# Expert layer on one Trainium2 core: two adds per turn moved to later search rounds, gathers queued ahead of scatters

## What is computed

```
def balanced_assignment(scores):          # scores: 8192 rows x 8 experts
    for e in range(E):
        s = jnp.where(taken, -jnp.inf, scores[:, e])
        _, idx = jax.lax.top_k(s, C)      # C = 1024 rows for each expert
        taken = taken.at[idx].set(True)
...
norm = layer_norm(feat, ln_g, ln_b)
sort_by_expert = balanced_assignment(norm @ centroids.T)
routed = feat[sort_by_expert].reshape(E, C, D)
h = layer_norm(routed, ln_g, ln_b)
h = gelu(einsum('ecd,edf->ecf', h, w1) + b1)      # D = 128, F = 512
h = einsum('ecf,efd->ecd', h, w2) + b2
out = routed + h                                   # back to the rows' places
```

## Time and profile before

| | us |
|---|---|
| median of 3 runs | 1326.44 (1326.17 to 1327.94) |
| the profiled execution, its own time | 1329.28 |
| its span in the trace (first to last instruction) | 1326.4 |
| PE busy | 1122.2 (85%) |
| DVE busy | 878.6 (66%) |
| POOL busy | 775.3 (58%) |
| ACT busy | 677.6 (51%) |
| mean granted TensorE clock | 0.914 of full |

### The profile page before, as it was taken

How to read it: one execution, slowest core, us unless ns; L and a number is a source line. 1 busy time by engine, 2 the same in 40 slices (tenths; PEclk the granted TensorE clock), 3 DMA queues, 4 the chain that set the end, 5 groups by cost and what they waited for, 6 DMA issues and landing times. The chain is left out here.

```text
span 1326.4 us, 34010 instructions
## 1 busy us (share of the span) xinstructions
PE 1122.2 (85%) x11612; PEld 734.3 (55%) x11612; DVE 878.6 (66%) x2747; ACT 677.6 (51%) x1452; POOL 775.3 (58%) x829
## 2 busy tenths in 40 slices
PE   4999999999999996647998994869999635999996
PEld 1444444444444443434776773759998324677674
DVE  7677777777777775777788602765556768777720
ACT  3777766777776764401433453575555400343353
POOL 2878887877888785102555674645554102466675
PEclk8999999999999998856999997879999755999998
DMA  8000000000000000410221223200000410122221
GB/s 193 2 1 0 0 0 0 0 0 0 0 0 0 0 1 2 144 33 21 60 58 56 79 72 95 59 1 0 0 0 0 135 42 19 47 61 61 61 84 40
DMA packets 55851, 47.32 MB, mean 36 GB/s; under 512 B 13142, under 2 KB 47190, under 8 KB 55772
## 3 DMA queue, kind: packets, MB, share of 16 engines
q1 hardware_dynamic: 44748, 27.92, 7.6%
q0 software_dynamic: 8192, 17.84, 4.8%
q10 hardware_dynamic: 2832, 0.54, 0.3%
HBM read 28.44 MB, written 17.83 MB: 35 GB/s over the span
## 5 line engine op out<-in xcount | busy, mean ns | idle before, releaser
L349 POOL TENSOR_TENSOR patt_aa<-patt_aa,causal_aa 128x512 f32<-128x512 f32 x256 | 319.3, 1274 | 73.4 <-DVE patt_aa L528 71.5
L528 DVE TENSOR_TENSOR patt_aa<-p_second_aa,first_aa 128x512 f32<-128x512 f32 x384 | 247.5, 686 | 133.9 <-ACT first_aa L424 130.5
L424 ACT ACTIVATE first_aa<-p_first_aa 128x512 f32<-128x512 f32 x384 | 208.6, 596 | 135.9 <-PE p_first_aa L627 132.1
L627 PE MATMUL p_second_aa<-q_t_aa,k_t_aa 32*128 32x512 f32 x768 | 234.8, 641 | 0.0
L627 PE MATMUL p_first_aa<-q_t_aa,k_t_aa 32*128 32x512 f32 x768 | 217.1, 641 | 15.1 <-ACT first_aa L424 14.8
L1423 POOL DMA_INDIRECT rows_e<-norm_rows,index_e x128 | 124.5, 973 | 163.7 <-DVE index_e L1119 126.5
L646 PEld LDWEIGHTS p_z_aa<-patt_aa,v_aa 128*32 128x32 f32 x3072 | 72.2, 109 | 147.5 <-issue 79.6
L1386 ACT ACTIVATE hid_e<-p_h_e,b_e 128x512 f32<-128x512 f32 x128 | 88.6, 692 | 116.3 <-PE p_h_e L1255 116.3
L1255 PE MATMUL p_h_e<-rows_t_e,w_e 128*128 128x512 f32 x256 | 144.5, 675 | 0.1
L1340 PE MATMUL p_cnt_e<-reach_e,ones_e 128*128 128x120 bf16 x896 | 84.6, 250 | 69.7 <-DVE reach_e L1183 69.5
L1376 ACT ACTIVATE rows_t_e<-p_t_e,bias,gain 128x512 f32<-128x512 f32 x32 | 24.9, 779 | 210.7 <-PE p_t_e L1246 210.7
(11 more groups left out here) (260 smaller groups left out, 2065.4 us busy)
## 6 DMA issues: line engine op xcount, KB each, us to landing
norm_rows<-norm_n SPq DMA_DIRECT2D x32, 288.0 KB, 2.8
w_e<-L_ffn_w SPq DMA_DIRECT2D x32, 256.0 KB
x<-L_attn_a_x SPq DMA_DIRECT2D x8, 512.0 KB, 5.4
x<-ffn_rows SPq DMA_DIRECT2D x7, 512.0 KB, 6.8
rows_e<-norm_rows,index_e POOLq DMA_INDIRECT x128, 2.6
ffn_rows<-yb_e,index_e POOLq DMA_INDIRECT x64
out<-yb_e,index_e POOLq DMA_INDIRECT x64
x<-ffn_rows SPq DMA_DIRECT2D x2, 256.0 KB, 3.2
```

The costliest lines, as they stand in the source:

```text
L349: pool.tensor_tensor(patt[n % LAG][:, b, :, :], patt[n % LAG][:, b, :, :], causal[:, None, :].broadcast_to([P, 4, P]), ALU.mult).then_inc( ...
L424: act.activation(first[n % 2][:, b, :], p_first[b][:], ACT.Identity).then_inc(first_copied, 1)
L528: dve.tensor_tensor(patt[n % LAG][:, b, :, :].rearrange("p h q -> p (h q)"), p_second[(2 * n + b) % ROOMS][:], first[n % 2][:, b, :], ALU. ...
L627: pe.matmul(out[:], k_t[par][rows, half, keys * P:(keys + 1) * P], q_t[par][rows, half, :, queries * P:(queries + 1) * P], start=True, sto ...
```

## The change

Two edits, both in `experts`. `add_back(e-3, 0)` goes from the window of round 2 to that of round 5 (the sixth), and `add_back(e-3, 1)` from round 4 to round 7 (the eighth). On GpSimd, a turn with one list does its gather first and its scatters behind it.

```
                     if e >= 3:
-                        windows[2].append(lambda: add_back(e - 3, 0))
-                        windows[4].append(lambda: add_back(e - 3, 1))
+                        windows[5].append(lambda: add_back(e - 3, 0))
+                        windows[7].append(lambda: add_back(e - 3, 1))
...
                 def turn(e, par, half):
                     _, lists, compute = does(e)
                     last = len(lists) > 1
+                    if lists and not last:
+                        gather(lists[0], 1 - par)
                     if compute and (not isinstance(e, int) or e > 2):
                         for h in range(2):
                             scatter(e - 3, 1 - par, half, h)
                             if last:
                                 gather(lists[h], lists[h] % 2)
-                    if lists and not last:
-                        gather(lists[0], 1 - par)
```

## The result

| | before | after |
|---|---|---|
| median, us | 1326.79 (1326.17 to 1327.94, 5 runs) | 1333.23 (1332.09 to 1334.29, 5 runs) |
| ratio to before | | 1.0044, 95% interval 1.0032 to 1.0055 |
| span of the profiled execution | 1326.4 | 1331.9 |
| PE, DVE, POOL busy, us | 1122.2, 878.6, 775.3 | 1121.2, 876.4, 772.2 |
| mean granted clock | 0.914 | 0.921 |

Measured again beside other executions of the kernel before (median 1325.64), the changed kernel took 1333.27 us: 1.0057, interval 1.0044 to 1.0070. So it is slower by 6 to 8 us, where 3.6 was forecast. The forecast's direction stands; the measured median lies 0.4 us above its range (the forecast started from a median of 1326.44, and 1.0044 times that is 1332.3, just inside).

What follows compares the result with a forecast made beforehand. Neither TensorE nor VectorE alone was taken to bound a searching turn; GpSimd's queue was nearly full from turn 6. Terms 0.05 + 0.23 + 0.3 + 2 x 1.5 gave 3.6 us slower, median 1330.0, range 1326.0 to 1332.8.

Steps and rivals of the forecast that it cites:

- Parts 1 and 2: Search turns: moving the adds from rounds 2 and 4 gains 0.60 and 0.20 us, so a turn lasts 26.09.
- Part 4: GpSimd's queue: twelve scatters between gathers of experts 5 and 6 delay turn 8; layers end 0.05 and 0.23 us later.
- Part 5: Scatters in rounds 1 and 2 slow VectorE: 0.04 us for each of eight turns, 0.3 in all.
- Part 6: TensorE's clock falls behind turn 8's wait of 3.4 us, costing 1.5 us in each layer.
- The sum: Whole kernel: the terms add to 3.6 us slower, span 1330.0 and median 1330.0.
- step from span to median: Whole kernel: a difference found in the traced span, 3.6 us, is added unchanged to the median of 1326.44.
- GpSimd's queue isn't the bound: Turn 8: expert 6's rows land within 34.9 us of expert 5's `index`, the gains stand, 1319.8 us; chance 0.06.
- GpSimd starves: Search: twelve scatters at 1.26 + 0.30 us each make expert 6 3.4 us later per layer, 1336.8; chance 0.04.
- The adds uncovered: Rounds 5 and 7: adds not hidden, a turn loses 1.2 and gains 0.8 us, 1333.2 in all; chance 0.05.

Runs made afterwards that it cites:

- turn-6 kernel: Kernel before, adds left in rounds 2 and 4, gather put ahead of the scatters in turn 6 alone: 1336.76 us, ratio 1.0083.
- turn 6 split: Changed kernel, but in turn 6 scatter half 0, gather, scatter half 1, with the first add in round 4: 1320.67 us, ratio 0.9965.
- order only: Kernel before, adds left in rounds 2 and 4, only GpSimd's order changed to gather first: 1340.28 us, ratio 1.0106.
- turn 6 as before: Changed kernel, with turn 6's adds and GpSimd order put back as in the kernel before: 1333.43 us, ratio 1.0039.
- adds only: Kernel before, only the adds moved to rounds 5 and 7, GpSimd's order kept: 1382.70 us, ratio 1.0428.
- wait filled: Changed kernel, plus 64 matmuls with unread results on TensorE ahead of turn 8's first transposes: 1329.62 us, ratio 1.0025.
- two split kernels: Changed kernel with the gather between the scatter halves and the first add in round 4, in turn 6 (1320.67 us) or turns 3 to 6 (1321.37 us).

## Why the prediction was right, and where its sizes were off

**Parts 1 and 2, the search.** Right. Turn 3, which has no scatters in its first rounds, lasts 26.06 for the 26.09 forecast, and VectorE's count in round 5 now waits for the add. The prediction credited the first layer's turns 3 to 5 with 2.68 us, though its own 0.80 a turn gives 2.40; they gained 2.46.

**Part 4, GpSimd's order.** The mechanism, the place and its being the bound were right; one term was short. From `index` of expert 5 to expert 6's transposes the second layer took 1279.77 - 1241.21 = 38.56 us, forecast 38.06:

| term, us | forecast | second layer |
|---|---|---|
| `index` to gather | 1.08 | 1.10 |
| eight gathers | 10.05 | 10.05 |
| twelve scatters | 15.35 | 16.06 |
| first to last gather | 8.98 | 8.79 |
| landing | 2.6 | 2.56 |

I had taken the scatter's 1.28 us from the earlier trace rows, where VectorE has nothing to do. Here VectorE lists expert 6 beside them: the scatter at 1252.36 took 1.39, and VectorE was then at `tile_of` (1252.19 to 1253.48); the one at 1264.36 took 1.15, beside the next list's `tile_of` (1263.97 to 1265.26). The first layer has the same picture: its longest scatter, 1.43 us, starts at 743.50 beside `tile_of` (743.37 to 744.66), and `index` to transposes takes 38.53. Twelve cost 0.7 us more than in the quiet stretch, and these two long scatters are 0.6 of it. The searches gave 0.25 less to `index` than forecast. Together that makes expert 6's transposes 0.77 and 0.99 us later than before (less what was there ahead of turn 3), where 0.05 and 0.23 stood.

**Part 5, contention.** 0.04 us a turn was too little: turns 4 and 5 last 0.15 us longer than turn 3, which differs in having no scatters in rounds 0 to 3. Set side by side, VectorE's timelines of turns 3 and 4 of the second layer part in three small steps (0.07 in round 1, 0.04 and 0.04 in round 3) and nowhere else; GpSimd's last scatter of that time starts 10.9 us into turn 4, in round 3. Round 1's `reach`, turn 3 and then turn 4, is the first step:

```profile
1150.31 0.73 DVE L1183 TENSOR_TENSOR reach_e<-high_of_e,cand_e 128x480 bf16<-128x480 uint16 x2
...
1176.37 0.79 DVE L1183 TENSOR_TENSOR reach_e<-high_of_e,cand_e 128x480 bf16<-128x480 uint16 x2
```

Of the Trainium skill's rule (SBUF — State Buffer, "SBUF: two separate sides") these runs again show the sign and not the size. The longest scatter of the changed kernel took 1429 ns, at most 0.46 us above the usual 969, and none the page's 3100:

```profile
L1430 POOL DMA_INDIRECT ffn_rows<-yb_e,index_e x64: 965/969/1429, 664.8 to 816.3; - x64
```

**Part 6, the clock.** Right in size: 1.50 and 1.45 us more between the transposes of experts 6 and 7, for 1.5 forecast. That it would fall was a judgement, and in part luck. It fell in all four waits of the two traces of the changed kernel, but the turn-6 kernel shows that it need not. The pause of the earlier trace rows, which was to show that 2 us are enough, did not lower the clock each time: in nine of the eleven traces it lasted 1.98 to 2.03 us, and the clock fell behind five of these and held behind four.

**The sum.** In layer times the change costs 2.27 + 2.44 = 4.7 us, where 3.6 were forecast; the 1.1 between them are two terms that were too small, the scatters' rate (15.35 for 16.06) and the contention (0.04 for 0.15 us a turn). The medians differ by more, 6.4 and 7.6. The profiled spans differ by 5.5: 4.7 in the layers, 0.2 between them, and 0.6 ahead of turn 3 of the first layer, where the change does nothing (the eleven traces reach that point anywhere from 634.7 to 637.1). A part of the rest may lie outside the expert layers too, in the very stretch of the earlier trace rows. That wait stands in the second attention, which no kernel here changes, and behind it the clock fell in some executions and held in others. The stretch behind the wait, in the changed kernel and in the kernel with turn 6 split:

```profile
852.87:856.87 4.00, 4.00 (x16) 3.62 (x15) 1.25 (x4) 2.00 (x5) 1.52 (x4) 0.57 0.00 0
```

```profile
846.34:850.34 4.00, 4.00 (x26) 3.90 (x25) 2.28 (x8) 3.08 (x9) 2.08 (x5) 1.00 0.01 4
```

The column "between" in the table above shows what it is worth: 355.77 to 356.22 us in the traces of before, after (both), order only and turn 6 as before, where this stretch was granted 0.57 or 0.58, and 353.53 to 354.71 in adds only, turn 6 only, wait filled and the two split kernels, where it was granted 1.00. The profiled execution of the kernel before had the fall. Its span, 1326.4, is above those of all its executions measured beside the experiments (1322.5 to 1326.2), so its median execution may have had none, while both traces of the changed kernel did. That would be 2 us of the difference, and the order-only kernel's 14.0 against 11.0 in its layers fits. This is argued and not shown: there is one trace for each measurement, and the spread ahead of turn 3 is as large. Whether the change makes this fall likelier, or chance did, stays open. It also means that the step from span to median, "a difference found in the span is added to either", was the weakest line of the sum.

**The rivals.** "GpSimd's queue isn't the bound" is refuted by the two waits for `rows` themselves. Its price was right: it is what happens when the stretch is made short enough, as in the kernel with turn 6 split, whose time was 1320.7, near the 1319.8 that the rival gave. (The rival's bound of 34.9 us should have been 34.7, 1272.56 - (1240.81 - 2.91), as TensorE and `index` both come earlier after the change.) "GpSimd starves" was the right direction for the missing term, at a fifth of its size. "The adds uncovered" gave 1333.2, the measured time to the tenth, but that is a coincidence: it is refuted by turn 3, which lasts 26.06 us and not the 27.3 that uncovered adds (26.9 + 1.2 - 0.8) would make of it.

## What to carry to other kernels

When work is put back in an in-order queue, count what then stands between two urgent pieces of it at the place where the queue has the least room, here the short turn at the end, and not in the steady state. Price the queue's instructions in the company that they will have there. Then list the second clients of what is late (the next user of its buffer) before choosing a new order: moving four scatters to the other side of one gather (and one add a round earlier) was worth 10.2 us in the layers and 12.6 by the medians; four others cost as much as they saved. And a wait on TensorE is priced with the slow stretch that may follow it, 1.4 to 1.5 us here, as a chance and not as a certainty.

## What the runs showed of the hardware

- Two waits of TensorE of nearly the same length (3.08 and 3.15 us) left the clock once at the lower level and once at the full one; two more, of 3.06 and 3.07, left it at the lower. A pause of 1.98 to 2.03 us in the second attention did either in different executions of unchanged code (lower in five, full in four). Length alone does not tell it in this range. Waits of 3.6 to 4.0 us all ended at the lower level (eight of eight), as did the eight of 6.4 to 7.6 us of the kernel with the adds only.
- Matmuls whose result nobody reads (64 of them, 3.52 us), put into such a wait, kept the clock at 1.0.
- In the changed kernel four scatters that started beside VectorE's `tile_of` took 1.14 to 1.43 us instead of 0.97, and turns with eight scatters in rounds 0 to 3 lasted 0.15 us longer. In the quiet stretch scatters start 1.28 us apart and gathers 1.25. The gathers landed 2.6 us after issue, the scatters 2.2 (medians).
